# The causal triangle on the diagonal score blocks: from four matrix products to VectorE's masked maximum

## What is computed

```python
def _L0_attn_ref(target, w_qkv, w_proj, b_proj, ln_gamma, ln_beta):
    B, T, D, H = (4, 256, 128, 16)
    HD = D // H
    NEG = 10000000000.0
    ...
    scores = jnp.einsum('bhqd,bhkd->bhqk', q, k) * (1.0 / np.sqrt(HD))
    causal = (jnp.arange(t)[:, None] >= jnp.arange(t)[None, :]).astype(scores.dtype)
    scores = scores * causal - (1.0 - causal) * NEG
    attn = jax.nn.softmax(scores, axis=-1)
    out = jnp.einsum('bhqk,bhkd->bhqd', attn, v)
    ...
```

## Time and profile before

| | us |
|---|---|
| median of 3 runs | 1314.72 |
| lowest, highest run | 1308.64, 1324.19 |
| profiled execution, device time | 1311.64 |
| its span, first to last instruction | 1309.8 |

### The profile page before, as it was taken

One profiled execution on the slowest core, in us unless ns is written; L12 is line 12 of the kernel. 1 busy time (PEld: TensorE's weight loads), 2 busy tenths in 40 slices (PEclk: granted clock), 3 DMA queues, 4 the chain that ended last, 5 costly groups with the idle time before them and its releaser, 6 DMA issues. The chain is left out here.

```text
span 1309.8 us, 30395 instructions
## 1 busy us (share of the span) xinstructions
PE 1246.0 (95%) x11960; PEld 454.0 (35%) x12022; DVE 1147.0 (88%) x1528; ACT 1061.3 (81%) x2064; POOL 183.0 (14%) x463
## 2 busy tenths in 40 slices
PE   7889999999999988999899999999999999999998
PEld 3253332332333352555223323333233332333454
DVE  6878989999999377766999999999999999998375
ACT  4657887898999946435599999999999999999641
POOL 9234221211111100112000000000000000000100
PEclk9999999999999999899999999999999999999999
DMA  5251310500000012002321000000000000000000
GB/s 135 57 141 45 50 19 20 63 5 13 4 3 3 5 42 65 1 1 73 97 61 43 3 4 13 4 4 3 13 4 4 4 3 13 4 4 2 13 9 25
DMA packets 38525, 35.11 MB, mean 27 GB/s; under 512 B 16080, under 2 KB 31920, under 8 KB 38384
## 3 DMA queue, kind: packets, MB, share of 16 engines
q1 hardware_dynamic: 38384, 33.17, 10.9%
HBM read 17.03 MB, written 9.70 MB: 20 GB/s over the span
## 5 line engine op out<-in xcount | busy, mean ns | idle before, releaser
L1583 DVE TENSOR_REDUCE m_blockmax<-ps 128x2 f32<-128x1024 f32 (+1 forms) x768 | 873.2, 1205 | 22.7 <-PE ps L1394 14.2
L1547 ACT ACTIVATE m_prob<-ps 128x512 f32<-128x512 f32 (+3 forms) x1664 | 849.0, 576 | 40.4 <-PE ps L1432 31.4
L1394 PE MATMUL ps<-m_k_all,m_q_all 64*128 64x512 bf16 (+2 forms) x1732 | 321.3, 376 | 16.4 <-DVE m_blockmax L1583 12.0
L1432 PE MATMUL ps<-m_q_max,m_k_all 64*128 64x512 bf16 (+3 forms) x1664 | 332.8, 366 | 0.5
L1455 PE MATMUL ps<-m_prob,m_v_op 128*9 128x256 f32 x4096 | 317.0, 381 | 0.1
L1394 PEld LDWEIGHTS ps<-m_k_all,m_q_all 64*128 64x128 bf16 x1732 | 82.0, 93 | 332.4 <-DVE m_blockmax L1583 225.1
L1451 PE MATMUL ps<-m_prob,m_v_op 128*9 128x256 f32 (+3 forms) x2560 | 177.9, 350 | 0.8 <-ACT m_prob L1547 0.3
L1432 PEld LDWEIGHTS ps<-m_q_max,m_k_all 64*128 64x128 bf16 x1664 | 147.1, 94 | 89.2 <-ACT m_prob L1547 36.6
L1606 POOL CAST m_maxparts<-m_negmax 128x8 bf16<-128x8 f32 x64 | 14.0, 218 | 703.4 <-DVE m_negmax L1562 698.3
L1455 PEld LDWEIGHTS ps<-m_prob,m_v_op 128*9 128x9 f32 x4096 | 60.9, 88 | 129.8 <-issue 117.7
L829 ACT ACTIVATE m_prob<-ps 128x512 f32<-128x512 f32 x40 | 23.8, 596 | 64.3 <-PE ps L692 54.3
(11 more groups left out here) (232 smaller groups left out, 966.7 us busy)
## 6 DMA issues: line engine op xcount, KB each, us to landing
m_part<-m_xn SPq DMA_DIRECT2D x48, 128.0 KB, 2.4
ba_parts<-m_part SPq DMA_DIRECT2D x8, 384.0 KB, 5.3
ea_parts<-m_part SPq DMA_DIRECT2D x8, 384.0 KB, 2.6
m_k_all<-ea_parts SPq DMA_DIRECT2D x84, 32.0 KB
m_q_all<-ea_parts SPq DMA_DIRECT2D x84, 32.0 KB
m_k_all<-ba_parts SPq DMA_DIRECT2D x36, 64.0 KB
m_q_all<-ba_parts SPq DMA_DIRECT2D x36, 64.0 KB
m_x<-in_x SPq DMA_DIRECT2D x4, 256.0 KB, 3.9
```

Of the source, the lines that this page charges most:

```text
L1394: mm = pe.matmul(ps[:, MX + 2 * (u % 2) + j, 0:width], q_all[head, pair, q0:q0 + TW], k_all[head, pair, CW * kc:CW * kc + width], start=Tr ...
L1432: pe.matmul(ps[:, e % ST, q0:CW], k_all[head, pair, TW * i:TW * i + TW], q_max[m % 2][head, q0:CW], start=True, stop=True).then_inc(self.s ...
L1547: nc.scalar.activation(prob[:, (2 * t + j) % NP, q0:CW], ps[:, e % ST, q0:CW], ACT.Exp, scale=SCALE)\
L1583: nc.vector.tensor_reduce(blockmax[:, m % plan.AHEAD, qt, :, kc], ps[:, MX + 2 * (u % 2):MX + 2 * (u % 2) + 2, 0:width], AX.X, ALU.max)\
```

## The change

VectorE's masked maximum is now used for all four query tiles of the own key block. `mask_q` grows from 256 to 512 columns, zero but for the triangle in the last 128, and `hidden`, where the masked sums are written, becomes two buffers, one for even and one for odd fills: the first where it was, the second new. TensorE's four mask products after the fills of qt 2 and 3 go, and with them `ident_h`, `hide_q` and the eight transfers that made them. The planner's costs change: no more 0.2 for the mask products on TensorE, and 0.25 + 2 width / 960 on VectorE for each own fill, where it was 0.45 for qt 0 and 1 and 0.11 for qt 2 and 3; so the order that it writes can change too.

```diff
--- before.py
+++ after.py
@@ -108,10 +108,8 @@
         k["id32"] = n.sb("id32", [P, 32], bf16)
         k["select"] = n.sb("select", [P, 2, 3, 2, P], bf16)
         k["max_ones"] = n.sb("max_ones", [P, 1], fp32)
-        k["mask_q"] = n.sb("mask_q", [P, 2 * TW], bf16)
-        k["hidden"] = k["sq"][:, 0:CW].bitcast(bf16).rearrange("p (u j w) -> p u j w", u=2, j=2)
-        k["ident_h"] = n.sb("ident_h", [P, 2, TW], bf16)
-        k["hide_q"] = n.sb("hide_q", [P, 2, TW], bf16)
+        k["mask_q"] = n.sb("mask_q", [P, CW], bf16)
+        k["hidden"] = [k["sq"][:, 0:CW].bitcast(bf16).rearrange("p (j w) -> p j w", j=2), n.sb("hidden", [P, 2, CW], bf16)]
         k["pick"] = n.sb("pick", [3 * EXPERTS, EXPERTS // 2, 2, ED], bf16)
         k["spread"] = n.sb("spread", [HALF, SUB, HEADS, HD], fp32)
         k["maxparts"] = n.sb("maxparts", [P, TPC, P], bf16)
@@ -173,16 +171,7 @@
 
     WEIGHTS_FOLDED, BIAS_FOLDED = 3, 4
 
-    def sp_halves(self, sp):
-        k = self.k
-        sp.wait_ge(self.made, self.IDENT_MADE)
-        for half, whole in (("ident_h", "identb"), ("hide_q", "mask_q")):
-            for j in range(2):
-                for h in range(2):
-                    sp.dma_start(k[half][HALF * j:HALF * j + HALF, h, :], k[whole][HALF * h:HALF * h + HALF, -TW:])\
-                        .then_inc(self.late_in, 16)
-
-    EARLY_IN, LORA_IN, LATE_IN = 16 * len(EARLY), 16 * len(LORA), 16 * (len(LATE) + 1 + 8)
+    EARLY_IN, LORA_IN, LATE_IN = 16 * len(EARLY), 16 * len(LORA), 16 * (len(LATE) + 1)
 
     def dve(self, dve):
         nc, k = self.nc, self.k
@@ -219,7 +208,7 @@
                            base=0, pattern=[[-1, P]], channel_multiplier=1)
         pool.affine_select(out=k["identb"][:, :], in_=k["identb"][:, :], compare_op=ALU.not_equal, fill=1.0,
                            base=0, pattern=[[-1, P]], channel_multiplier=1)
-        pool.affine_select(out=k["mask_q"][:, TW:], in_=k["mask_q"][:, TW:], compare_op=ALU.is_ge, fill=MASK,
+        pool.affine_select(out=k["mask_q"][:, CW - TW:], in_=k["mask_q"][:, CW - TW:], compare_op=ALU.is_ge, fill=MASK,
                            base=0, pattern=[[-1, TW]], channel_multiplier=1)
         pool.affine_select(out=k["id32"][:, :], in_=k["id32"][:, :], compare_op=ALU.not_equal, fill=1.0,
                            base=0, pattern=[[-1, 32]], channel_multiplier=1).then_inc(made, 1)
@@ -1117,9 +1106,9 @@
                 m, g = self.steps[f]
                 width = self.fills(m)[g][2]
                 order.append(("fill", m, g))
-                own, late = self.fills(m)[g][1] == self.windows[m][1], self.fills(m)[g][0] >= 2
-                tensor = first + 0.08 + width / 3500.0 + (0.2 if own and late else 0.0)
-                vector = max(vector, tensor + 0.2) + (0.45 if own and not late else 0.11) + 2 * width / 960.0
+                own = self.fills(m)[g][1] == self.windows[m][1]
+                tensor = first + 0.08 + width / 3500.0
+                vector = max(vector, tensor + 0.2) + (0.25 if own else 0.11) + 2 * width / 960.0
                 f += 1
                 if g == self.keys(m) - 1:
                     maxed[m] = vector
@@ -1393,12 +1382,6 @@
                     head = slice(HALF * j, HALF * j + HALF)
                     mm = pe.matmul(ps[:, MX + 2 * (u % 2) + j, 0:width], q_all[head, pair, q0:q0 + TW],
                                    k_all[head, pair, CW * kc:CW * kc + width], start=True, stop=True)
-            if causal and kc == c and qt >= 2:
-                for h in range(2):
-                    for j in range(2):
-                        head = slice(HALF * j, HALF * j + HALF)
-                        mm = pe.matmul(ps[:, MX + 2 * (u % 2) + j, width - TW:width], k["ident_h"][head, h, :],
-                                       k["hide_q"][head, h, :], start=False, stop=True, skip_group_check=True)
             mm.then_inc(self.mx_filled, 1)
 
         def turn_max(m):
@@ -1572,11 +1555,11 @@
             u = plan.fill_no[m, f]
             qt, kc, width = plan.fills(m)[f]
             dve.wait_ge(self.mx_filled, u + 1)
-            if self.causal and kc == plan.windows[m][1] and qt < 2:
+            if self.causal and kc == plan.windows[m][1]:
                 for j in range(2):
                     reduce = nc.vector.tensor_tensor_reduce(
-                        k["hidden"][:, u % 2, j, 0:width], ps[:, MX + 2 * (u % 2) + j, 0:width],
-                        k["mask_q"][:, 2 * TW - width:], 1.0, LOWEST, ALU.add, ALU.max,
+                        k["hidden"][u % 2][:, j, 0:width], ps[:, MX + 2 * (u % 2) + j, 0:width],
+                        k["mask_q"][:, CW - width:], 1.0, LOWEST, ALU.add, ALU.max,
                         blockmax[:, m % plan.AHEAD, qt, j, kc:kc + 1])
                 reduce.then_inc(self.mx_used, 1)
             else:
@@ -1765,7 +1748,6 @@
             def _(sp):
                 constants.sp(sp)
                 ffn_a.sp(sp)
-                constants.sp_halves(sp)
                 att_b.sp(sp)
                 ffn_c.sp(sp)
                 att_e.sp(sp)
```

## The result

| | before | after |
|---|---|---|
| median, us | 1313.68 | 1326.99 |
| lowest, highest | 1308.21, 1324.19 | 1322.22, 1334.43 |
| runs | 20 | 20 |
| span of the profiled execution | 1309.8 | 1321.0 |

The ratio of after to before is 1.0095, 95% interval 1.0077 to 1.0113: the change makes the kernel 13 us, about 1%, slower. The forecast was 1313 us with a range to 1322; the time lies above the range.

What follows compares the result with a forecast made beforehand. No single engine was the bound; round trips between VectorE and TensorE set the period. Terms +0.2 - 0.7 - 0.3 + 1.2 + 0.2 = +0.6 us gave 1312.2 on the profiled execution, put at 1313 us, range 1304 to 1322.

Steps and rivals of the forecast that it cites:

- The order: TensorE's planned order: turn and seventh fill keep their place in c=3; c=1 may change; taken as 0, with bounds.
- The fifth case: Rival, slower: turn after the seventh fill in c=1, TensorE waiting for ScalarE's copy, up to 0.6 us a window; chance 0.10.
- the sum: Setup and the four stages of the attention loop together: +0.2 - 0.7 - 0.3 + 1.2 + 0.2 = +0.6 us.
- forecast -0.04: Stage c=1 round trip: one fill's mask products save 0.12, the 512-wide fill adds 0.08; -0.3 us in the stage.
- the removal buys nothing there and the addition is paid whole: Stage c=2: VectorE's added work counts, removed mask products do not; 0.155 us a window, +1.2 in the stage.
- forecast +0.02: Stage c=3: a VectorE wait of some 0.1 us goes and pays for most of the added 0.16; +0.2 in all.
- forecast -0.7: Stage c=0: shorter VectorE waits behind mask products give 1.9 us, the 16 changed fills add 1.2.
- Setup: POOL clears a 512-column mask tile before TensorE's first product: +0.2 us; the eight removed SyncE transfers bring 0.
- The masked maximum: VectorE's masked reduces at 384 and 512 columns, 553 and 688 ns by extrapolation; 5.0 us more VectorE work in all.
- TensorE pacing alone: Rival for the attention loop: TensorE's queue is the only limit and the whole 7.7 us come back, 1305.5; chance 0.20.
- VectorE as the bound: Rival, slower: every added VectorE instruction is paid and nothing returned, +5.0 + 0.2, 1318 us; chance 0.14.
- the order closes the waits: Rival: the new order removes all 19.2 us of VectorE's waits less 5.0 of work, 14.2 us, 1299; chance 0.06.

Runs made afterwards that it cites:

- The first experiment: The changed kernel with the planner's two cost lines as before, so the new arithmetic in the old order: 1312.26 us, ratio 0.9976 to the kernel before.
- the first two experiments: New arithmetic in the old order, 1312.26 us; and the kernel before with only the planner's cost lines changed, so in the new order, 1327.89 us.
- the maximum without mask: New arithmetic in the old order, with each row's maximum taken over hidden scores too, as one plain instruction: 1308.62 us, ratio 0.9938 to the kernel before.
- the base: The changed kernel with the planner's old cost lines, so the new arithmetic in the old order: 1312.26 us, ratio 0.9976 to the kernel before.
- the pair alone: New arithmetic in old order, c=3 reordered: two steps together at a window's end, turn ahead of the last step; ratio 0.9996 to the kernel before.
- the two with the early turn: New arithmetic, planner's old costs, turn due earlier in c=1 and c=2: 1312.83 us, ratio 0.9965; then in c=3 too: ratio 0.9984, both to before.

## Why the prediction was wrong

**The step that failed is "The order".** It took 0 for the order and kept "same place" for c=3. It compared two due times, that of the turn and that of the seventh fill, from VectorE's planned costs. For these two it was mostly right: in the kernel after the turn is still ahead of the seventh fill in all windows of c=2 and in five of the eight of c=3. The planner has a third thing to place, the steps, and a second figure that I named but didn't carry through: TensorE's planned time no longer had 0.2 in it for each of two fills. Both figures enter into what is due first at each of the 33 places of a window of c=3, and a step that comes early shifts all after it. In c=1, where I saw the danger, nothing moved from the third window on; in its first two the turn did go behind the seventh fill, and they took 9.08 and 8.24 us, against 9.12 and 9.05 in the old order. In c=2 and c=3 steps ran ahead by one and stood in pairs, and these stages took +4.9 and +9.4 us. The sentence "I am wrong ... if the order in c=1 and c=2 shifts by more than one place" pointed at this; the order in c=2 did shift, and c=3, where the larger part was lost, is missing in it.

**The fifth case named the right kind of cause, but not the one that cost most.** It had the turn behind one more fill and TensorE waiting for the copy, up to 0.6 us a window: measured alone in c=3, 0.64. It was put in c=1, with "it alone decides for slower by over 1% only if c=3 joins". In the kernel after that turn comes in every other window of c=3, TensorE does wait 0.45 us for the copy, and VectorE waits 0.17 behind it, no more than in the old order. Most of the loss stands behind something the prediction had no term for, the pairs of steps: 0.44 and 0.67 of the 1.3 us a window (one pair alone, 0.50). So that its 1323 us is near the measured time is luck. Its 0.10 also rested on an order that could be worked out from the lines of the planner before any run, and wasn't.

**What was priced from rows held.** The first experiment is the change with an unchanged order, as the sum supposed. It gave 1312.26 us against 1313, and a span of 1309.7 against 1309.8 + 0.6; but executions of one kernel spread over some 15 us, so that closeness is partly luck. The forecast of 1313 to the 1314.72 of before is 0.9987, inside the interval of 0.9948 to 1.0003 around 0.9976; the sum of +0.6 us by itself is 1.0005, just outside it. The windows test the terms better:

- c=1: forecast -0.04 a window on a period of 9.03; measured 8.94, -0.09, the right way and twice the size.
- c=2: forecast +0.155, "the removal buys nothing there and the addition is paid whole"; measured +0.15 (13.15 to 13.30; the 13.21 of the prediction is the mean with the first windows of the stage).
- c=3: forecast +0.02; measured +0.02 (17.55 to 17.57).
- c=0: forecast -0.7; measured 28.66 from its first to its last join (85.92, 114.58) against 29.22, -0.6; the kernel after has -1.5, the rest with its new order.
- Setup: forecast 5.3 for TensorE's first product; it starts at 5.29.
- The masked maximum: forecast 553 and 688 ns; measured 550 and 683. The page VectorE: DVE Perf Modes of the Trainium skill (section "The TRN2 errata") gives 120 cycles beside the columns, by which I estimate 0.66 us from start to start at 512 columns. The trace stays below the rule: the first experiment's time line has the two starts at 380.80 and 381.40, 0.60 apart.

**The other rivals.** TensorE pacing alone (1305.5) fell: c=3 stayed at 17.57. VectorE as the bound (1318) fell by the first two experiments, and by the maximum without mask, where only part of its saving came back. That the order closes the waits (1299) went the other way: waits grew from 13.2 to 20.8 us.

**Why so small a change of order costs so much.** In c=3 the base has VectorE busy 17.25 of 17.56 us and TensorE's queue nearly as full; the two hand over two bank pairs in strict turn (17.25: the stretch 364.57 to 382.13 of that kernel, with TensorE's products at 17.36). VectorE idles 0.3 us in a window. Its work doesn't depend on the order (17.22 to 17.32 us in windows of four orders, the base's among them), so as I read it a gap of 0.4 or 0.8 us in the supply of fills can take the place of at most that 0.3, and the rest is added to every window: with the pair alone 0.81 us of named waits stand against the base's 0.20, and the window is 0.50 longer.

## What to carry to other kernels

Where a program's order is computed from planned costs, an edit of a cost is an edit of the order: work the whole new order out and compare it place by place before adding up any saving of work. Where two engines hand over few buffers in turn, each 95 to 98% busy by the profile, the order can be worth more than the work removed; here 13 us against the 7.7 us that the prediction counted in TensorE's queue for the products. And when work moves, try it in the old order first: that one experiment told work and order apart.

## What the hardware showed that I had not expected

TensorE's clock fell in one place in the trace of the new arithmetic and not in that of the kernel before, the order being the same. The second window of c=3 has few steps, and TensorE waits a lot in it. The stretches of the kernel before (columns as above, the clock is the third figure from the right):

```profile
315.00:317.00 2.00, 1.25 (x10) 0.60 (x11) 1.93 (x7) 0.41 (x1) 0.00 (x0) 1.00 0.00 0
317.00:319.00 2.00, 2.00 (x24) 0.54 (x24) 2.00 (x2) 1.52 (x4) 0.00 (x0) 1.00 0.00 0
```

and of the new arithmetic in the same order:

```profile
315.00:317.00 2.00, 1.47 (x8) 0.69 (x9) 1.93 (x7) 0.00 (x0) 0.00 (x0) 0.63 0.01 4
317.00:319.00 2.00, 1.85 (x14) 0.33 (x12) 2.00 (x2) 1.10 (x3) 0.00 (x0) 0.52 0.00 0
```

The granted clock of 0.63 and 0.52 means the lower level, 1.2 GHz, for most of four microseconds; it is back at 2.4 from 319 on; in the two microseconds ahead of this, 313 to 315, TensorE had been busy for 1.08 us, and for 1.09 in the kernel before, whose clock held. The turn's four products take 0.63 us there instead of 0.39, and the window takes 18.36 us where it took 17.54. The same window has a mean clock of 0.91 in eight further kernels of this study, and 0.81 and 0.82 in the two with the early turn. In one of the eight, the old arithmetic in the new order, the products were still there; the kernel after has 1.00 and 17.72 us. So the removed products alone don't decide the clock. In the second window of c=2 it even differs where nothing else does: 0.87 in the first experiment's kernel (13.43 us), and 1.00 in three kernels that have its arithmetic and its order up to there (12.84 and 12.85 us). With one trace of each kernel, the cause stays open. At 0.8 us in one window it decides nothing here, but that is about what the eight windows of c=1 won by the arithmetic.
